# A cross-attention-and-MoE layer: softplus off VectorE, one ring of expert matrices, gate products in the routing tail

## The reference

```python
# part 1: a selective scan over the context, gated by the normalized x
xin = einsum('bld,ed->bel', ctx, in_proj_w)             # 256 -> 512 channels
u   = silu(causal_conv4(xin, conv_w) + conv_b)          # per channel
dt_low, Bm, Cm = split(x_proj_w @ u)                    # 16, 16, 16 rows
dt  = softplus(dt_proj_w @ dt_low + dt_proj_b)          # [b, 512, L]
state = state * exp(dt * A) + (dt * u) * Bm             # over L, 16 states a channel
y   = sum_n(state * Cm) + D * u
x   = x + (y * silu(layernorm(x))).T
# part 2: a mixture of experts on h = layernorm(x), 2048 tokens
score = softmax(h @ gate_w.T); top 6 of 64 experts; at most 64 tokens an expert
y_e = (silu(h_e @ w_gate[e]) * (h_e @ w_up[e])) @ w_down[e]       # 512 -> 352 -> 512
out = x + sum over chosen experts of score * y_e
        + (silu(h @ sw_gate) * (h @ sw_up)) @ sw_down             # shared, 512 -> 704 -> 512
```

## Time and profile before

| | |
|---|---|
| median of 3 runs | 1228.05 us (1227.44 to 1231.49) |
| profiled execution | 1226.79 us |
| its span | 1225.0 us |
| TensorE / VectorE / ScalarE / GpSimd busy | 933 / 690 / 475 / 626 us |
| moved | 246 MB |

### The profile page before, as it was taken

The page is one execution under the profiler, slowest core; times in us unless marked ns, Lnnn a source line. Parts: engine busy times, 40 slices in busy tenths (PEclk is TensorE's granted clock), DMA queues, the critical chain, the costliest instruction groups (busy, mean ns, idle before and its releaser), DMA issues. The chain is left out here.

```text
span 1225.0 us, 12116 instructions
## 1 busy us (share of the span) xinstructions
PE 933.4 (76%) x4037; PEld 504.7 (41%) x4037; DVE 690.1 (56%) x884; ACT 474.9 (39%) x729; POOL 626.2 (51%) x331
## 2 busy tenths in 40 slices
PE   5345635467889667898579994589999999997797
PEld 2143334364444454444455443334444444443342
DVE  3397897999889999788988752211111211211111
ACT  3546543475755465665464602211111111111111
POOL 0597699975897857798857910112121112122211
PEclk9667666577988669998759995689999999998999
DMA  8331334243333423332225627299999999999993
GB/s 307 105 121 69 131 111 138 95 133 104 105 103 104 146 82 104 140 137 104 104 97 162 231 90 300 99 334 343 347 348 353 355 364 353 358 353 357 345 345 69
DMA packets 75733, 246.38 MB, mean 201 GB/s; under 512 B 11740, under 2 KB 14312, under 8 KB 75416
## 3 DMA queue, kind: packets, MB, share of 16 engines
q1 hardware_dynamic: 63512, 222.01, 51.3%
q0 software_dynamic: 7744, 18.88, 6.4%
q10 hardware_dynamic: 4416, 4.72, 1.1%
HBM read 226.41 MB, written 19.17 MB: 200 GB/s over the span
## 5 line engine op out<-in xcount | busy, mean ns | idle before, releaser
L538 PE MATMUL ps<-ident,arena 128*128 128x128 f32 (+1 forms) x1408 | 253.6, 337 | 200.6 <-POOL arena L1265 92.6
L538 PEld LDWEIGHTS ps<-ident,arena 128*128 128x128 f32 (+1 forms) x1408 | 213.4, 182 | 309.0 <-issue 117.8
L1260 POOL TENSOR_TENSOR arena<-arena 128x1024 f32<-128x1024 f32 x128 | 303.8, 2393 | 6.7 <-PE ps L538 5.6
L857 ACT ACTIVATE ps<-arena,An 128x511 f32<-128x511 f32 x256 | 165.1, 680 | 188.6 <-DVE ps L1023 122.0
L1265 POOL TENSOR_TENSOR arena<-arena 128x1024 f32<-128x1024 f32 x64 | 152.6, 2385 | 118.4 <-DVE arena L1015 114.7
L1284 POOL DMA_INDIRECT out_rows<-xn,idxs x32 | 50.9, 1590 | 311.7 <-ACT xn L786 167.2
L705 PE MATMUL ps<-arena 128*64 128x352 f32 x1024 | 173.6, 496 | 0.0
L1015 DVE TENSOR_TENSOR_SCAN ps<-ps,arena 128x1024 f32<-128x1024 f32 x64 | 146.3, 2285 | 7.5 <-POOL arena L1260 5.1
L1015 DVE TENSOR_TENSOR_SCAN arena<-ps,arena 128x1024 f32<-128x1024 f32 x64 | 146.1, 2283 | 4.4 <-POOL arena L1260 3.7
L1170 DVE TENSOR_TENSOR arena<-arena,ps 128x352 f32<-128x352 f32 x32 | 16.7, 521 | 227.2 <-ACT arena L929 227.2
L667 PE MATMUL ps<-xnT,sw 128*128 128x512 f32 (+1 forms) x288 | 133.7, 604 | 4.8 <-DVE hs L1066 4.7
(11 more groups left out here) (143 smaller groups left out, 1000.0 us busy)
## 6 DMA issues: line engine op xcount, KB each, us to landing
arena<-bc_rows SPq DMA_DIRECT2D x128, 512.0 KB, 4.6
arena<-in_L_ffn_w_gate SPq DMA_DIRECT2D x64, 704.0 KB, 14.3
arena<-in_L_ffn_w_up SPq DMA_DIRECT2D x64, 704.0 KB, 16.8
arena<-in_L_ffn_w_down SPq DMA_DIRECT2D x64, 512.0 KB, 10.8
arena<-in_L_ffn_w_down SPq DMA_DIRECT2D x64, 192.0 KB, 11.3
arena<-in_x SPq DMA_DIRECT2D x4, 1024.0 KB, 6.8
xn_rows<-xn ACTq DMA_DIRECT2D x16, 256.0 KB, 3.8
out_rows<-arena SPq DMA_DIRECT2D x4, 1024.0 KB, 6.7
```

What stands on the lines that cost most here:

```text
L538: return nc.tensor.matmul(dst, src, ident[0:k, 0:k], is_transpose=True, **kw)
L857: a = nc.scalar.activation(ps[:, 2 * (c % 2) + n, 1:L], dt[k][:, 1:L], ACT.Exp, scale=An[:, k, NB * g + n:NB * g + n + 1])
L1260: G.tensor_tensor(R[c % RING], dtu[k][:, None, :].to_broadcast([P, NB, L]), Brep[n % REPS], ALU.mult)\
```

## The change

- **Softplus** becomes relu(x) + log(1 + exp(-|x|)), with the same correction: on ScalarE `xdt` (Abs and Relu), `exp` (Exp, then + 1), `ln` (Ln, then - 1 and - ln 1); on GpSimd three additions `c`, `sp`, `dt`, then `dtu` as before. Nothing of it is left on VectorE.
- **Small steps** of the layer norms (`znorm`, `xnorm`: exp(-0.5 ln(var + eps))), of the top score (`negm`) and of the softmax (`norm`) go to ScalarE; the cast and subtraction of `places` to GpSimd. Sums over earlier batches (`csum`) are made by more matmuls.
- **Tables:** `log_and_exp()` loads the set with both Ln and Exp after each group of SiLUs; SiLUs stand in groups (4 `u`, 4 `zs`, 6 `ssilu`).
- **Weigh:** steps 6, 14 and 22 of each batch are weighed by VectorE too.
- **Shared products** of earlier batches: all gate products (copied into `hs` by `scopy`), then six SiLUs in place, then all up products, then down, closer together.
- **Tail:** four `xn` buffers with one store; logits a quarter at a time; one-hot slots a quarter at a time; five of six gate products of the last batch stand between `logits`, `pos`, `table`, `sel` and the first tokens; 11 shared pieces over 28 turns.
- **Weights:** a ring of 20 places of one matrix; a down matrix comes as 112 rows of 6 KB and 16 of 2 KB, and the hidden rows are put in that order by two multiplications. A load waits for the products of the matrix 20 before it.

The diff, cut to what matters here:

```diff
-        homes = [arena[:, j * PAIRW:(j + 1) * PAIRW] for j in range(SLOTS - 1)] + [sw[:]]
+        slots = [arena[:, n * SLOT:(n + 1) * SLOT] for n in range(6)] + [extra[:]]
+        slots += [arena[:, n * SLOT:(n + 1) * SLOT] for n in range(6, ASLOTS)]
...
         def by_vector(q):
-            return q % 2 == 1
+            return q % 2 == 1 or q % STEPS in (6, 14, 22)
...
-                        add(r + 0.7, "dve", "xm", b, k)
-                        add(r + 0.95, "act", "exp", b, k)
-                        add(r + 2.0, "act", "du", b, k)
-                        add(r + 1.2, "pool", "round", b, k)
-                        add(r + 1.6 - 0.25 * h, "act", "ln", b, k)
-                        add(r + 2.65, "dve", "softplus", b, k)
-                        add(r + 3.1, "pool", "dtu", b, k)
-                        r += 0.3
+                        add(r + 0.75, "act", "exp", b, k)
+                        add(r + 1.2, "act", "ln", b, k)
+                        add(r + 1.75, "pool", "c", b, k)
+                        add(r + 2.35, "pool", "sp", b, k)
+                        add(r + 2.75, "pool", "dt", b, k)
+                        add(r + 3.35, "pool", "dtu", b, k)
+                        add(r + 1.75, "act", "du", b, k)
+                        r += 1.7
...
+            for c in range(NI - 1):
+                BANK["sgate", B - 1, c] = c % 2
+                add(last[c], "pe", "sgate", B - 1, (c, 0))
+                add(last[c] + 0.01, "pe", "sgate", B - 1, (c, 1))
+                add(last[c] + (0.5 if c < 2 else 6.0), "act", "scopy", B - 1, c)
             for b in range(B - 1):
-                t = after[b]
+                t = after[b] + 0.3
                 for c in range(NI):
-                    t = grab(("sgate", b, c), t, 1.6)
+                    t = grab(("sgate", b, c), t, 1.3)
                     add(t, "pe", "sgate", b, (c, 0))
-                    add(t + 0.6, "pe", "sgate", b, (c, 1))
-                    add(t + 1.3, "act", "ssilu", b, c)
-                    t = grab(("sup", b, c), t + 1.0, 1.9)
+                    add(t + 0.5, "pe", "sgate", b, (c, 1))
+                    add(t + 1.0, "act", "scopy", b, c)
+                    t += 0.65
+                t = math.ceil(t + 0.6) + 0.71
+                for c in range(NI):
+                    add(t + 0.005 * c, "act", "ssilu", b, c)
+                for c in range(NI):
+                    t = grab(("sup", b, c), t, 1.6)
                     add(t, "pe", "sup", b, (c, 0))
-                    add(t + 0.6, "pe", "sup", b, (c, 1))
-                    add(t + 1.55, "dve", "shs", b, c)
-                    t += 1.0
-                t += 0.9
+                    add(t + 0.5, "pe", "sup", b, (c, 1))
+                    add(t + 1.25, "dve", "shs", b, c)
+                    t += 0.8
+                t += 0.8
...
-        ITEMS = [("up", c) for c in range(NI)] + [("down", c) for c in range(LT)]
-        OVER = NPAIR
+        ITEMS = [("gate", NI - 1)] + [("up", c) for c in range(NI)] + [("down", c) for c in range(LT)]
+        OVER = 28
...
+                if what == "down":
+                    w = w_down[2 * q + e]
+                    load(dst[0:ROWS], w[0:3 * ROWS].rearrange("(p c) h -> p c h", c=3), sm)
+                    load(dst[ROWS:P, 0, :], w[3 * ROWS:I], sm)
...
+            for n in range(SLOTS, len(PIECES)):
+                what, q, e = PIECES[n - SLOTS]
+                sp.wait_ge(s[{"gate": "eg_mm", "up": "eu_mm", "down": "y2_mm"}[what]], q + 1)
+                piece(n)
...
+                elif kind == "scopy":
+                    m, n = ISC[c], NI * b + c
+                    act.wait_ge(s["sg_mm"], n + 1)
...
+                    copy(hs[0:m, c, :], ps[0:m, BANK["sgate", b, c], :], s["sg_ready"])
```

More of the change, by code:

```diff
@@ L38 @@
 XBS = 3
+ASLOTS = 19
 RW = H + E
@@ L84, in build @@
         du = [carve(L) for _ in range(2)]
-        zs = [carve(L) for _ in range(2)]
+        zs = [carve(L) for _ in range(LT)]
         assert at[0] == EARLY
@@ L306, in first_phase @@
+                for k in range(DC):
+                    t = grab(("zT", b, k), t + 0.4, 0.5)
+                    add(t, "pe", "zT", b, k)
+                    add(t + 0.25, "act", "zT", b, k)
                 s0 = STEPS * (b + 1)
@@ L365, in first_phase @@
             t = STEPS * B
-            for n in range(PIECES):
+            for n in range(7):
                 add(t - 13 + n, "sp", "piece", 0, n)
-                add(t + 2.3 + 0.01 * n, "sp", "piece", 1, n)
-                add(t + 2.4 + 0.01 * n, "sp", "piece", 2, n)
+            for n in range(7, 10):
+                add(t - 0.4 + 0.01 * n, "sp", "piece", 0, n)
+            for n in range(10, SLOTS):
+                add(t + 2.3 + 0.01 * n, "sp", "piece", 0, n)
             parts.sort()
@@ L532, in claim @@
             def claim(bank):
+                if bank < 4 and bank not in freed:
+                    pe.wait_ge(s["scan_done"], NQ)
+                    weighed(pe, NQ - 1)
                 for sm, n in freed.get(bank, ()):
@@ L557, in _ @@
                 i = DC * b + c if isinstance(c, int) else None
-                bank = BANK.get((kind, b, None if kind == "table" else c))
+                bank = BANK.get((kind, b, None if kind in ("table", "logits") else c))
                 if kind == "ctx":
@@ L631, in _ @@
                             nc.tensor.matmul(dst, ones[:], mask[:, k, :], start=False, stop=False)
-                        if b >= 1:
-                            nc.tensor.matmul(dst, ones[:], csum[:], start=False, stop=False)
+                        for k in range(b):
+                            nc.tensor.matmul(dst, ones[:], msum[k][:], start=False, stop=False)
                         nc.tensor.matmul(dst, ones[0:1, :], iota_b[0:1, :], start=False, stop=True)
@@ L695, in gate_up_mm @@
             def gate_up_mm(q):
-                j = HOME[q]
                 pe.wait_ge(s["xgT_ready"], q + 1)
-                for n in range(4):
-                    pe.wait_ge(w_in[j][n], 16 * USES[q])
-                if q:
-                    pe.wait_ge(s["h_ready"], q)
-                for n in range(2):
+                for n, what in enumerate(("gate", "up")):
+                    for e in range(2):
+                        loaded(pe, what, q, e)
+                    if q:
+                        pe.wait_ge(s["silu_ready" if n == 0 else "h_ready"], q)
                     for k in range(HC):
@@ L720, in down_mm @@
             def down_mm(q):
-                j, w = q % 2, HOME[q]
+                j = q % 2
                 pe.wait_ge(s["hT_ready"], q + 1)
-                for n in range(4, PIECES):
-                    pe.wait_ge(w_in[w][n], 16 * USES[q])
+                for e in range(2):
+                    loaded(pe, "down", q, e)
                 if q >= 2:
@@ L759, in shared @@
                     mm.then_inc(s["sdn_mm"], 1)
-            pe.wait_ge(s["scan_done"], NQ)
-            weighed(pe, NQ - 1)
+            for bank in range(4):
+                claim(bank)
             tokens(0)
```

586 lines of the change are left out of this document (316 added, 270 removed).

## The result

The changed kernel takes 1272.8 us (median of 4; 1264.5 to 1320.4) against 1227.7 for the kernel before. The ratio is 1.034 with a 95% interval of 1.028 to 1.040: slower, where I had forecast 1142 and a gain. The ratio leaves one disturbed execution of the changed kernel out. The profiled execution took 1264.45 us for a span of 1262.6.

The account below looks back on a forecast made before the run. VectorE was taken to pace the scans first, TensorE part of each later batch and the experts. 1226.8 + 1.5 (start) - 52 (scans) - 9 (tail) - 26 (experts) = 1141.3 us profiled, 1142 as median; range 1090 to 1195.

Parts of the forecast that it names:

- the part on weights: Expert weight loads: ring costed at nothing; 6 KB rows land the gathers sooner, 4 of 33 us gained (bounds 0 and 20).
- The ring itself: Weight buffers in the experts: no cost, since weights are never waited for and slack of a whole pair covers them.
- Experts otherwise: Experts besides the 6 KB rows: -17.6 us for gate products leaving, -4 for fewer token waits and a down product.
- Softplus and VectorE's relief: Scan stage: VectorE sheds net 82.5 us, leaving 500, priced at mean times in the stage; first batch gains 21.
- Bunches: Scan stage: six SiLUs in a row on ScalarE delay dA; two bunches hit in full, 7 us (bounds 0, 40).
- the rival *Bunches: Denser products make TensorE stop the scans, 30 us lost, and the tail at half clock, +15: 1187 us, chance 0.18.
- The scans in sum: First scan to last xstats: 21 + 15 + 15 + 8 - 7 = 52 us gained (bounds 10 and 82).
- Tail: From xstats to first expert product, 50 us before: -9 us; +6 at half clock, -15 without any product ahead.
- The slower rival: Scan stage: 18 gate copies ahead of dA on ScalarE each wait a whole product; 95 us more, 1237 us, chance 0.06.
- The signs of being wrong: Scans: dA waits behind a copy or SiLUs, TensorE's clock falls, VectorE idles over 100 us; or TensorE waits for weights.

## Why the prediction was wrong, step by step

- **The step that failed** is in the part on weights: "Rows of 6 KB mean fewer packets; they can only help by landing the gathers sooner: 4 of 33 (bounds 0 and 20)". I counted packets and not partitions, and took the lower bound as 0 although nothing excluded a loss. Measured: +76 us (506.1 against 430.3), where I had -4. The trace of before had a sign that I did not read: its 96-row transfers of 192 KB took 11.3 us to land, as long as the 128-row ones of 512 KB (10.8). It is no proof, since the one may have stood behind the other, but it called for a bound on the side of a loss. The second step that failed is "The ring itself is costed at nothing: weights are never waited for". With the old rows, at 331 GB/s for 326, TensorE still waits 17.4 us for down matrices.
- **Experts otherwise:** -22 forecast without the 6 KB rows, -11.9 measured (430.3). TensorE's busy time fell by 16.9 (397.1 to 380.2), near what I had priced, but its idle time rose by 5.0: the wait for tokens fell by 16.8, and weights are waited for instead. The five gate products, priced at 17.6, are worth 6.0. I saw a DMA share of 0.96 in the earlier trace rows and did not make transfers a rival bound; that was the second error.
- **Softplus and VectorE's relief:** the mechanism held. VectorE was busy 493.7 us up to the last xstats, 500 forecast; the relief was that of the means in the stage, not the smaller one that the undisturbed times of VectorE gave. The size of the gain did not: the first batch gained 13.5 us for 21 forecast, because GpSimd, at 127 of 141 us, had become a pacer: the scans wait 12.2 us for it there, less with more weightings moved. An addition there took 1.27 us, near the price taken.
- **Bunches:** priced at 7 us in all with 40 as the bound; putting the old order back gave 19. I looked at ScalarE's side of them, but the bunch acted through TensorE and then through VectorE's queue (38.6 us of waits for up products, for 23.3). This is the place and sign of the rival *Bunches*, and about two thirds of its 30 us.
- **The scans in sum:** 22.7 for 52. Of the 29 missing, the products' order is 19 (shown). With the old order the gains are 13.4, 2.4 and 10.3 us in the first three batches, where I had 21, 15 and 15, and 13.8 from there to the last xstats, where I had 8, less 7 for bunches. So after the first batch it is the second and third that fell short, where the scans wait for `dA`; that this wait is the reason is not shown.
- **Tail:** -4.2 for -9. The products ahead of pos, beside places and ahead of the first tokens took 5.8, 6.9 and 8.8 us, at a granted clock of 0.61, 1.00 and 0.81. Taking all of them out gave 4.8, where I had said 6, so their term was right. What fell short is the rest of the tail: 41.0 without any product is 9 below the 50.0 of before, not 15. Up to the last logit it is 8.7 shorter (16.1 for 24.8), where I had 10.9; from there on only 0.3, so one-hot slots a quarter at a time gained nothing that can be seen.

```profile
726.73 5.78 PE ps L695 x8
...
734.40 6.87 PE ps L695 x16
...
744.78 8.77 PE ps L695 x16
```

- **The slower rival,** 18 gate copies ahead of dA, did not come as a time: the scans got faster. Its mechanism is in the trace all the same, at a part of its 95 us: the scans wait 39.8 us for dA in all, for 3.2 before. The kernel is slower for a reason that was in none of my rivals.
- **The signs of being wrong:** three of the four came. dA waits behind a copy, VectorE's idle time is 161 us for 79, and TensorE waits for weights. TensorE's clock in the scans did not fall (0.80 for 0.79).

## What to carry to other kernels

Choose a transfer's layout by partitions first: here loads to all 128 of them ran at 392 to 409 GB/s whether a row had 4, 5.5 or 6 KB, and those to 112, 96 or 64 at 204 to 279, and in the kernel the layout cost three times what these rates add up to. Before TensorE's work is moved for a gain, look at the DMA share of the stretch; at 0.96 to 1.00, much of the freed TensorE time becomes waiting for transfers. And products planned as densely as one engine can take them stop the engines whose queues hold their evictions, and what stands behind these; a third of a step more between them was worth 14 us.

## What was unexpected of the hardware

- 112 rows of 5632 B at 279 GB/s, 128 rows at 409; 96 rows of 6144 B at 260; 64 rows at 204, on the first or the last 64 partitions alike.
- With the changed down rows the rate depends on which matrices are read (281 GB/s for pairs 10 to 19, 331 for pairs 0 to 9, both at 20 in flight), and on the former it is 335 with 7 in flight. On pairs 0 to 9 (331 at 20, 356 at 7) the difference is hardly above the scatter. With 128 and 96 rows in the mix depth made no such difference (376 at 20 in flight, 367 at 7, on other matrices).
- The gate matrices, whose rows are the same throughout, took 14.3 us to land before, 21.0 with all of the change but the down rows, and 28.6 with these.
